# Audio tower with sparsemax attention and top-k experts: one refinement over eight rows, one flag per pair, and a reordered way from the last residual to the first gather

## The chip, the core and the metric

The kernel runs on one core of a Trainium2 chip. The metric is the device time of one launch in microseconds (us), of which three runs are given as a median with their lowest and highest. The engines are called as in the profile: PE (TensorE), DVE (VectorE), ACT (ScalarE), POOL (GpSimd) and SP (SyncE). They run side by side and meet at semaphores.

## What is computed

x is 16 x 64 x 750. Each channel is cut into patches of 200 samples; magnitudes and phases of their spectra go through two dense layers, which gives h, 16 sequences of 256 tokens of width 128. Then:

```python
h = tok(x)                                            # 16 x 256 x 128
h = h + attn(layernorm(h))                            # 8 heads of 64
h = h + ffn(layernorm(h))

def sparsemax(z):                                     # over the 256 scores of a row
    z_sorted = flip(sort(z)); cssv = cumsum(z_sorted)
    k = sum(1.0 + r * z_sorted > cssv)                # r = 1..256: size of the support
    tau = (cssv[k - 1] - 1.0) / k
    return maximum(z - tau, 0.0)

def ffn(x):                                           # 4096 tokens, 8 experts
    probs = softmax(x @ Wr, axis=0)                   # over the tokens
    vals, idx = top_k(probs.T, 1024)                  # 1024 tokens for each expert
    h = gelu(einsum(x[idx], W1) + b1)
    out_e = einsum(h, W2) + b2
    return zeros.at[idx].add(vals * out_e)
```

## The kernel before, in words

**Attention.** The 4096 tokens are worked on in G = 8 groups of 512, that is two sequences. One round of the attention (`attention_round`, one function per engine) does the scores, thresholds and outputs of one group and prepares the next. The order of a round is written out by hand: `PLAN` for PE and ACT, `STEPS` for DVE. A group has 8 score blocks `sc[0]` to `sc[7]`, each 128 x 4 x 256: 128 partitions, 4 rows (two heads by two tiles of tokens), 256 scores. Two blocks make a *pair* d (0 to 3), so a pair holds eight rows per partition, and each block is one *half* u of four rows. There are 32 pairs in all.

For a pair DVE does three steps. `largest` takes the 8 largest scores of each row. `thresholds` takes these out, finds the next 8, sums up the 16, and gets from them the threshold `tau` (128 x 8). In most places the first `largest` instructions of the following pair are laced into it (`laced_thresholds`). This `tau` is right if no more than 16 scores of the row lie above it. A row where the 16th largest score lies above `tau` may need more. `thresholds` therefore ends with three instructions (L1099 to L1102, or L1068 to L1071): a compare into `above`, and two reduces into `more`, one flag for each half and one for the pair. POOL takes the maximum of the three over the partitions (`anymore`, L457), which goes to `more_all`. The third step, `settle` (L1184), loads the pair's flag into a register. If it is zero, DVE goes straight to `minus_tau` (L1205), for which ACT waits before its relu (L646); PE transposes the result of the relu (L829, "turn"). If the flag is not zero, `refine` chooses a half by the flag of half 1, copies its four thresholds to `tau_u`, and `surplus` (L1108) adds up relu(score - tau) over each of the four rows, takes the largest sum over all partitions, and sets `go` if it is over 1 by more than 3e-6. The sum of both half flags stands in `go_5`, so that `go` is also set when both halves are flagged. If `go` is set, `rest` does a Newton step (`newton`: counts the scores above tau, corrects tau, calls `surplus` again), repeats it while `go` is set, copies the thresholds back, and if both halves are flagged goes over the other half with `passes`:

```python
v.tensor_tensor(go_5[0:1, 4:5], more_all[0:1, d, 0:1], more_all[0:1, d, 1:2], ALU.add)
u = v.value_load(more_all[0:1, d, 1:2], min_val=0, max_val=1)
```

**From the last residual to the first gather.** The last group's second norm (`second_norm`, `layernorm`), on DVE with one power on POOL, sends `xn2` to PE, which makes the router's logits. DVE then does the softmax over tokens with POOL, fills some constants (L1319 to L1324), and finds for each expert the 1024th largest probability by 15 steps of two bits (`two_bits`), each with a trip to PE that counts (`total`). A last `total` counts the elements above the threshold (`gt`); `ranks` goes to PE twice, for the elements equal to it (`eq`) and for the chosen ones (`sel`). `one_hots` makes from an expert's ranks a matrix `lo_hot` (128 x 32 x 128) and `hi_val`, PE multiplies them (`expert_slots`, L911), and `slots` turns the product into token numbers `gather_at` and weights `slot_w`.

**Experts.** POOL gathers 1024 rows for an expert by eight indirect DMAs (L506) and adds its results into the output by eight more (L519); the order on its queue is gather 0, 1, 2, scatter 0, and then in turn. PE does the two dense layers (L933, L947), ACT the gelus, DVE the bias and the weights (`weighted`). SP loads the experts' weights before.

## Time and profile before

| | us |
|---|---|
| median of 3 runs (lowest to highest) | 903.33 (898.98 to 903.69) |
| the profiled execution | 908.21 |
| its span | 906.4 |
| PE busy in it | 682.0 (75%) |
| DVE busy | 605.2 (67%) |
| ACT busy | 456.9 (50%) |
| POOL busy | 207.0 (23%) |

The span runs from the first to the last instruction of the execution that was profiled. "Busy" adds up the instructions of one engine. Of all these shares none says what a stage waits for; that is read from the waits and the timeline of each stage. In the rows below, a number in square brackets is the time in which the engine did nothing before the instruction, with the one that ended it; "issue" means that the profile shows nothing that was waited for. Times of a timeline count from the span's start.

### The profile page before, as it was taken

How to read it: one execution, taken by the hardware profiler on the slowest of the kernel's cores; microseconds unless marked ns; L12 is line 12 of the kernel's file. 1: busy time of each engine (PE TensorE's matmuls, PEld its weight loads, DVE VectorE, ACT ScalarE, POOL GpSimd, SP SyncE). 2: the span in 40 equal slices, each digit the busy share in tenths (PEclk: the TensorE clock that was granted, in tenths of full speed). 3: DMA queues.
4: the chain of work that ended last, by engine and by line, in shares of the span. 5: the costliest groups of instructions: out<-in, count | busy, mean ns of one | idle time of the engine just before them, and what ended most of it. 6: DMA issues, size and time to landing. Idle time of an engine off the chain costs nothing. (4 is left out here: it accounts for less than half of the span.)

```text
span 906.4 us, 13135 instructions
## 1 busy us (share of the span) xinstructions
PE 682.0 (75%) x4060; PEld 449.3 (50%) x4060; DVE 605.2 (67%) x2215; ACT 456.9 (50%) x664; POOL 207.0 (23%) x212
## 2 busy tenths in 40 slices
PE   5598679679989997499999998663322996667890
PEld 3254265356565574275575765452211665544570
DVE  2868887588868868788877889846888455432110
ACT  3958638357766764478778777652000231222120
POOL 1000010001000010010010010002005588888776
PEclk9889989889999999699999998895555897779895
DMA  5200000000000000000000000005001153344333
GB/s 156 80 1 1 1 1 1 1 2 13 2 3 13 2 2 13 2 2 13 2 13 3 1 13 1 13 1 157 0 0 33 38 87 43 63 69 69 68 33 29
DMA packets 34722, 23.69 MB, mean 26 GB/s; under 512 B 8232, under 2 KB 31226, under 8 KB 34628
## 3 DMA queue, kind: packets, MB, share of 16 engines
q0 software_dynamic: 11264, 8.40, 6.9%
q1 hardware_dynamic: 23152, 14.21, 5.6%
q8 instruction: 28, 0.46, 0.2%
q14 instruction: 66, 0.54, 0.2%
q10 hardware_dynamic: 212, 0.08, 0.0%
HBM read 14.29 MB, written 8.39 MB: 25 GB/s over the span
## 5 line engine op out<-in xcount | busy, mean ns | idle before, releaser
L549 ACT ACTIVATE front<-ps 128x1024 f32<-128x1024 f32 x128 | 127.8, 1026 | 37.2 <-PE ps L796 13.3
L646 ACT ACTIVATE front<-front,minus_tau 128x256 f32<-128x256 f32 x256 | 108.6, 497 | 57.6 <-DVE minus_tau L1205 56.4
L549 ACT ACTIVATE back<-ps 128x1024 f32<-128x1024 f32 x72 | 73.7, 1024 | 82.6 <-PE ps L920 68.5
L457 POOL CROSS_LANE_REDUCE more_all<-more 128x3 int32<-128x3 f32 x32 | 15.2, 475 | 429.0 <-DVEq L1103 290.9
L829 PE MATMUL ps<-ident,front 128*128 128x128 f32 x512 | 77.0, 300 | 47.4 <-ACTq L648 22.9
L519 POOL DMA_INDIRECT out_dram<-back x64 | 102.6, 1603 | 27.4 <-issue 20.2
L549 ACT ACTIVATE back<-ps,back 128x1024 f32<-128x1024 f32 x32 | 35.4, 1114 | 130.2 <-remote 59.3
L829 PEld LDWEIGHTS ps<-ident,front 128*128 128x128 f32 x512 | 65.0, 154 | 70.2 <-issue 37.4
L947 PE MATMUL ps<-back 128*128 128x128 f32 x512 | 68.4, 300 | 22.3 <-ACT back L549 20.3
L506 POOL DMA_INDIRECT back<-rows,back x64 | 63.5, 992 | 75.6 <-issue 71.3
L947 PEld LDWEIGHTS ps<-back 128*128 128x128 f32 x512 | 66.2, 214 | 26.3 <-issue 26.3
L1077 DVE MATCH_REPLACE8 back<-top,front 128x256 f32<-128x256 f32 x176 | 69.7, 409 | 0.0
L845 PE MATMUL ps<-back,front 128*64 128x256 f32 x512 | 68.5, 396 | 1.3 <-ACT back L549 1.2
L819 PE MATMUL ps<-front 64*128 64x256 f32 x512 | 67.3, 398 | 2.0 <-issue 1.2
L933 PE MATMUL ps<-back 128*128 128x512 f32 x128 | 63.4, 637 | 6.8 <-issue 3.6
L1046 DVE MAX8 top<-front 128x8 f32<-128x256 f32 x168 | 58.7, 413 | 10.0 <-issue 5.9
L1080 DVE MAX8 top<-back 128x8 f32<-128x256 f32 x176 | 59.7, 411 | 1.6
L796 PE MATMUL ps<-xcur,wqkv 128*128 128x512 f32 x128 | 58.7, 611 | 2.0 <-ACT front L572 1.3
L819 PEld LDWEIGHTS ps<-front 64*128 64x128 f32 x512 | 47.5, 191 | 16.5 <-issue 10.2
L751 PE MATMUL ps<-back,w1m 101*128 101x512 f32 x96 | 52.7, 632 | 2.3 <-issue 2.3
L769 PE MATMUL ps<-w2t,hid 128*128 128x128 f32 x384 | 46.9, 284 | 9.1 <-ACT hid_r L607 7.6
L450 POOL TENSOR_TENSOR rstd<-var_eps,minus_half 128x4 f32<-128x4 f32 x16 | 19.5, 1219 | 145.5 <-DVE var_eps L360 145.5
(191 smaller groups left out, 1092.8 us busy)
## 6 DMA issues: line engine op xcount, KB each, us to landing
back<-in_L_ffn_W_dram SPq DMA_DIRECT2D x16, 256.0 KB
front<-in_x_dram SPq DMA_DIRECT2D x4, 750.0 KB, 4.5
rows<-xn SPq DMA_DIRECT2D x8, 256.0 KB, 2.2
out_dram<-h SPq DMA_DIRECT2D x1, 2048.0 KB, 7.8
back<-rows,back POOLq DMA_INDIRECT x64
out_dram<-back POOLq DMA_INDIRECT x64
wqkv<-in_L_attn_W_qkv_dram SPq DMA_DIRECT2D x1, 768.0 KB, 6.0
back<-in_L_ffn_b_dram SPq DMA_DIRECT2D x8, 64.0 KB
```

Of the source, the lines that this page charges most:

```text
L506: g.indirect_dma_start(xg[p][:, s, :], None, rows2[:, :], bass.IndirectOffsetOnAxis(ap=gather_at[p][:, s:s + 1], axis=0))\
L519: g.indirect_dma_start(orow[:, :], bass.IndirectOffsetOnAxis(ap=add_at[p][:, s:s + 1], axis=0), y[p][:, s, :], None, compute_op=ALU.add)\
L549: a.activation(dst, ps[s][:, 0:cols], func, **kw).then_inc(sems[f"free{s}"], 1)
L646: a.activation(prob[n % 2][:, r, :], sc[n][:, r, :], ACT.Relu, bias=minus_tau[:, n // 2, n % 2 * 4 + r:n % 2 * 4 + r + 1])
L796: last = mm(o[:, q * 512:(q + 1) * 512], wqkv[:, m * P:(m + 1) * P], xcur[:, :], start=True, stop=True)
L819: last = mm(o[:, a_ * 512 + it * SEQ:a_ * 512 + (it + 1) * SEQ], z[r, hp, b * SEQ + it * P:b * SEQ + (it + 1) * P], z[r, 4 + hp, b * SEQ:( ...
L829: last = nc.tensor.transpose(o[:, a_ * 512 + jb * SEQ + it * P:a_ * 512 + jb * SEQ + (it + 1) * P], prob[n % 2][:, 2 * a_ + it, jb * P:(jb ...
L845: last = mm(o[a_ * DH:(a_ + 1) * DH, hp * SEQ:(hp + 1) * SEQ], v_sb[p][:, 2 * b + jb, hd * DH:(hd + 1) * DH], prob_t[n % 2][:, 2 * a_ + jb ...
L933: last = mm(o[:, q * 512:(q + 1) * 512], ew1[p][:, m * P:(m + 1) * P], xg_t[:, q * 512:(q + 1) * 512], start=True, stop=True)
L947: last = mm(o[:, s * D:(s + 1) * D], eh[:, k, s * P:(s + 1) * P], ew2[p][:, k, :], start=(k == 0), stop=(k == F // P - 1))
L1077: v.match_replace(sc2[:, r, :], top[d % 2][:, r, 0:8], sc[2 * d + r // 4][:, r % 4, :], LOWEST)
L1080: last = v.max(top[d % 2][:, r, 8:16], sc2[:, r, :])
```

## The change

Three things change. (1) The refinement works on all eight rows of a pair at once, on `tau` itself; the half flags, `tau_u`, `twice` and `passes` go, and one flag per pair is made with the compare. `go` now depends on the row sums alone. (2) Between the last residual and the logits, the norm's statistics of the first two tiles are taken before the last residual, and the constants are filled before the wait for the logits. (3) The count of `gt` rides with the first trip of `ranks`; the first expert's `lo_hot` is made last and in four quarters, each of which releases eight matmuls; `slots` writes the token numbers as integers at once and flags them before the weights are added.

```diff
@@ -894,20 +892,26 @@
-total(3 * BITS // 2, [gt])
 for n, m in enumerate((eq, sel)):
     t_.wait_ge(sems["rk_in"], n + 1)
     job = c.job(0)
     o = slot(job)
+    if m is eq:
+        rows = o[:, E * NT:E * (NT + JB)].rearrange("p (r j) -> p r j", j=JB)
+        for j in range(0, NT, JB):
+            mm(rows, ones[:, :], gt[:, :, j:j + JB], start=(j == 0), stop=(j + JB == NT))
     mm(o[:, 0:E * NT], not_before[:, :], m[:, :, :].rearrange("p e j -> p (e j)"), start=True, stop=True)
     done(job, mm(o[:, 512:512 + E * NT], ones[:, :], m[:, :, :].rearrange("p e j -> p (e j)"),
                  start=True, stop=True))

-def expert_slots(e):
-    t_.wait_ge(sems["hot_ok"], e + 1)
+def expert_slots(e, first=False):
+    if not first:
+        t_.wait_ge(sems["hot_ok"], e + 1)
     job = c.job(3)
     o = slot(job)
     for j in range(NT):
+        if first and j % (NT // 4) == 0:
+            t_.wait_ge(sems["hot_quarter"], j // (NT // 4) + 1)
         last = mm(o[:, 0:5 * CT], lo_hot[:, j, :], hi_val[:, j, :, :].rearrange("p v s -> p (v s)"),
                   start=(j == 0), stop=(j == NT - 1))
     done(job, last)
@@ -1096,19 +1098,14 @@
-    v.tensor_tensor(above[:, :], top[d % 2][:, :, 15], tau[:, d, :], ALU.is_gt)
-    v.drain()
-    v.tensor_reduce(more[:, d, 0:2], above[:, :].rearrange("p (u r) -> p u r", r=4), AX.X, ALU.max)
-    v.tensor_reduce(more[:, d, 2:3], above[:, :], AX.X, ALU.max)
+    v.scalar_tensor_tensor(above[:, :], top[d % 2][:, :, 15], 1.0, tau[:, d, :], ALU.mult, ALU.is_gt,
+                           accum_out=more[:, d, :])
     v.drain().then_inc(sems["more_ok"], 1)

-def half(d, u, r):
-    return sc_d[d][:, ds(u, 1), r, :].rearrange("p u n -> p (u n)")
-
-def surplus(d, u):
-
-    for r in range(4):
-        v.scalar_tensor_tensor(sc2[:, r, :], half(d, u, r), tau_u[:, r:r + 1],
+def surplus(d):
+
+    for r in range(8):
+        v.scalar_tensor_tensor(sc2[:, r, :], sc[2 * d + r // 4][:, r % 4, :], tau[:, d, r:r + 1],
                                zero[:, :].to_broadcast([P, SEQ]),
                                ALU.subtract, ALU.max, accum_out=r_sum[:, r:r + 1])
     v.drain()
@@ -1119,18 +1116,18 @@
     v.tensor_reduce(go_s[:, 0:1], go_t[:, :], AX.X, ALU.max)
     v.drain()
     for k in range(4):
-        v.tensor_copy(go_5[0:1, k:k + 1], go_s[32 * k:32 * k + 1, 0:1])
-    v.drain()
-    v.tensor_reduce(go_s[0:1, 0:1], go_5[0:1, :], AX.X, ALU.max)
+        v.tensor_copy(go_4[0:1, k:k + 1], go_s[32 * k:32 * k + 1, 0:1])
+    v.drain()
+    v.tensor_reduce(go_s[0:1, 0:1], go_4[0:1, :], AX.X, ALU.max)
     v.drain()
     v.tensor_scalar(go[0:1, :], go_s[0:1, 0:1], -1.0, 3e-6, ALU.add, ALU.is_gt)
     v.drain()

-def newton(d, u):
-
-    for r in range(4):
-        v.tensor_scalar(sc2[:, 4 + r, :], half(d, u, r), tau_u[:, r:r + 1], None, ALU.is_gt, ALU.add,
-                        accum_out=r_cnt[:, r:r + 1])
+def newton(d):
+
+    for r in range(8):
+        v.tensor_scalar(sc2[:, r, :], sc[2 * d + r // 4][:, r % 4, :], tau[:, d, r:r + 1], None,
+                        ALU.is_gt, ALU.add, accum_out=r_cnt[:, r:r + 1])
     v.tensor_scalar(r_sum[:, :], r_sum[:, :], -1.0, None, ALU.add)
     v.drain()
     v.tensor_scalar(r_cnt[:, :], r_cnt[:, :], 1.0, None, ALU.max)
@@ -1139,44 +1136,24 @@
     v.drain()
     v.tensor_tensor(r_cnt[:, :], r_sum[:, :], r_cnt[:, :], ALU.mult)
     v.drain()
-    v.tensor_tensor(tau_u[:, :], tau_u[:, :], r_cnt[:, :], ALU.add)
-    v.drain()
-    surplus(d, u)
+    v.tensor_tensor(tau[:, d, :], tau[:, d, :], r_cnt[:, :], ALU.add)
+    v.drain()
+    surplus(d)

 def go_on():
     return v.value_load(go[0:1, 0:1], min_val=0, max_val=1) > 0

-def passes(d, u):
-
-    mine = tau[:, d, ds(u * 4, 4)]
-    v.tensor_copy(tau_u[:, :], mine)
-    v.drain()
-    surplus(d, u)
+def rest_of_refinement(d):
+
+    newton(d)
     with v.If(go_on()):
-        with v.Fori(0, 26):
-            with v.If(go_on()):
-                newton(d, u)
-            v.drain()
-        v.tensor_copy(mine, tau_u[:, :])
-        v.drain()
-
-def rest_of_refinement(d, u):
-
-    v.memset(go_5[0:1, 4:5], 0.0)
-    newton(d, u)
-    with v.If(go_on()):
-        newton(d, u)
+        newton(d)
         with v.If(go_on()):
             with v.Fori(0, 24):
                 with v.If(go_on()):
-                    newton(d, u)
+                    newton(d)
                 v.drain()
             v.drain()
-    v.tensor_copy(tau[:, d, ds(u * 4, 4)], tau_u[:, :])
-    v.tensor_tensor(twice[0:1, :], more_all[0:1, d, 0:1], more_all[0:1, d, 1:2], ALU.mult)
-    v.drain()
-    with v.If(v.value_load(twice[0:1, 0:1], min_val=0, max_val=1) > 0):
-        passes(d, 0)
     v.drain()

 settled = Tally(None)
@@ -1186,20 +1163,16 @@
     v.wait_ge(sems["anymore_ok"], c.up("anymore_ok"))
     v.sem_inc(sems["held"], 1)
     n = settled.up()
-    wide = v.value_load(more_all[0:1, d, 2:3])
+    wide = v.value_load(more_all[0:1, d, :])
     hint = ahead.pop()
     if more_follow:
         ahead.append(v.mark_branch_hint_location())
     v.br_ne(wide, 0, f"refine{n}", f"settled{n}").branch_hint(hint)
     with nc.body(f"refine{n}", valid_engines=[mybir.EngineType.DVE]):
-        v.tensor_tensor(go_5[0:1, 4:5], more_all[0:1, d, 0:1], more_all[0:1, d, 1:2], ALU.add)
-        u = v.value_load(more_all[0:1, d, 1:2], min_val=0, max_val=1)
-        v.tensor_copy(tau_u[:, :], tau[:, d, ds(u * 4, 4)])
-        v.drain()
-        surplus(d, u)
+        surplus(d)
         v.br_ne(v.value_load(go[0:1, 0:1], min_val=0, max_val=1), 0, f"rest{n}", f"settled{n}")
     with nc.body(f"rest{n}", valid_engines=[mybir.EngineType.DVE]):
-        rest_of_refinement(d, v.value_load(more_all[0:1, d, 1:2], min_val=0, max_val=1))
+        rest_of_refinement(d)
         v.br(f"settled{n}")
     nc.switch_bb(f"settled{n}")
     v.tensor_scalar(minus_tau[:, d, :], tau[:, d, :], -1.0, None, ALU.mult).then_inc(sems["tau_ok"], 1)
@@ -1297,8 +1270,35 @@
 attention_round(G - 2, ("hid", "emb"))
 attention_round(G - 1, BEFORE, last=True)
 jobs = {(k, n): job for k, n, job in walk(c, END)}
+half_done = h[:, (G - 1) * 4:G * 4, :]
+v.drain()
+for j in range(2):
+    v.bn_stats(stats[:, j, :], half_done[:, j, :])
+v.drain()
+for j in range(2):
+    v.bn_aggr(mv[:, j, :], stats[:, j, :])
 residual(jobs["out", 1], G - 1, 1)
-second_norm(G - 1, v.drain)
+v.drain()
+for j in range(2, 4):
+    v.bn_stats(stats[:, j, :], half_done[:, j, :])
+v.drain()
+for j in range(2, 4):
+    v.bn_aggr(mv[:, j, :], stats[:, j, :])
+v.drain()
+v.tensor_scalar(var_eps[:, :], mv[:, :, 1], EPS, None, ALU.add).then_inc(sems["ve_ok"], 1)
+v.wait_ge(sems["rows_out"], (G - 1) * 16 + 1)
+v.sem_inc(sems["held"], 1)
+v.wait_ge(sems["rstd_ok"], c.up("rstd_ok"))
+for j in range(4):
+    last = v.tensor_scalar(xn2[:, j, :], half_done[:, j, :], mv[:, j, 0:1], rstd[:, j:j + 1],
+                           ALU.subtract, ALU.mult)
+last.then_inc(sems["xn2_ok"], 1)
+v.memset(seg32[:, :, 1:NT], 1.0)
+v.tensor_copy(iota_b[:, :], iota_r[:, :])
+v.memset(seg32[:, :, 0:1], 0.0)
+for k in range(4):
+    v.memset(nexts[:, k, :], k << (BITS - 2))
+    v.memset(steps4[:, k, :], k << (BITS - 4))
 emptied(jobs["logit", 0])


@@ -1362,19 +1356,18 @@
 thr_b = nexts[:, 0, :].bitcast(f32).unsqueeze(2).to_broadcast([P, E, NT])
 v.tensor_tensor(gt[:, :, :], pr[:, :, :], thr_b, ALU.is_gt)
 v.tensor_tensor(eq[:, :, :], pr[:, :, :], thr_b, ALU.is_equal)
-v.drain().then_inc(sems["cnt_in"], 1)
-filled(c.job(0))
-add_up(above_thr[:, :], E)
-v.drain()
-
-v.tensor_scalar(wanted[:, :], above_thr[:, :], -1.0, float(CAP), ALU.mult, ALU.add)

 def ranks(mask):

     v.drain().then_inc(sems["rk_in"], 1)
     filled(c.job(0))
+    if mask is eq:
+        v.tensor_reduce(above_thr[:, :], ps[0][:, E * NT:E * (NT + JB)].rearrange("p (r j) -> p r j", j=JB),
+                        AX.X, ALU.add)
     v.tensor_tensor_scan(flat(rank), flat(seg32), ps[0][:, 512:512 + E * NT], 0.0, ALU.mult, ALU.add)
     v.drain()
+    if mask is eq:
+        v.tensor_scalar(wanted[:, :], above_thr[:, :], -1.0, float(CAP), ALU.mult, ALU.add)
     v.tensor_tensor(flat(rank), flat(rank), ps[0][:, 0:E * NT], ALU.add).then_inc(sems["free0"], 1)
     v.drain()

@@ -1404,9 +1397,6 @@
     v.drain()
     hi = hi_f[:, ds(e, 1), :].rearrange("p e j -> p (e j)")
     va = vals[:, ds(e, 1), :, :].rearrange("p e j n -> p (e j) n")
-    if first:
-        v.tensor_tensor(lo_hot[:, :, :], iota_b[:, :].unsqueeze(1).to_broadcast([P, NT, P]),
-                        lo_e[:, :].unsqueeze(2).to_broadcast([P, NT, P]), ALU.is_equal)
     for j in range(0 if first else NT):
         v.tensor_scalar(lo_hot[:, j, :], iota_b[:, :], lo_e[:, j:j + 1], None, ALU.is_equal)
     v.tensor_tensor(hi_hot[:, :, :], iota_r[:, 1:CT + 1].unsqueeze(1).to_broadcast([P, NT, CT]),
@@ -1414,6 +1404,11 @@
     v.drain()
     v.tensor_tensor(hi_val[:, :, :, :], hi_hot[:, :, :].unsqueeze(2).to_broadcast([P, NT, 5, CT]),
                     va.unsqueeze(3).to_broadcast([P, NT, 5, CT]), ALU.mult)
+    for q in range(4 if first else 0):
+        rows = slice(q * NT // 4, (q + 1) * NT // 4)
+        v.tensor_tensor(lo_hot[:, rows, :], iota_b[:, :].unsqueeze(1).to_broadcast([P, NT // 4, P]),
+                        lo_e[:, rows].unsqueeze(2).to_broadcast([P, NT // 4, P]), ALU.is_equal)
+        v.drain().then_inc(sems["hot_quarter"], 1)
     v.drain().then_inc(sems["hot_ok"], 1)

 def slots(n, p, first=False):
@@ -1422,16 +1417,16 @@
     job = c.job(3)
     free(job, v.tensor_copy(parts[:, :, :].rearrange("p v s -> p (v s)"), filled(job)[:, 0:5 * CT]))
     v.drain()
-    v.scalar_tensor_tensor(slot_f[:, :], parts[:, 0, :], float(P), parts[:, 1, :], ALU.mult, ALU.add)
-    v.tensor_tensor(parts[:, 2, :], parts[:, 2, :], parts[:, 3, :], ALU.add)
-    v.drain()
-    v.tensor_copy(slot_i[:, ds(e, 1), :].rearrange("p e s -> p (e s)"), slot_f[:, :])
     if not first:
         v.wait_ge(sems[f"xg_in{p}"], n * (16 * CT))
-    v.tensor_copy(gather_at[p][:, :], slot_f[:, :])
+    v.scalar_tensor_tensor(gather_at[p][:, :], parts[:, 0, :], float(P), parts[:, 1, :], ALU.mult, ALU.add)
+    v.drain().then_inc(sems["slots_ok"], 1)
+    v.tensor_tensor(parts[:, 2, :], parts[:, 2, :], parts[:, 3, :], ALU.add)
+    v.tensor_copy(slot_i[:, ds(e, 1), :].rearrange("p e s -> p (e s)"), gather_at[p][:, :])
+    v.drain()
     v.tensor_tensor(slot_w[:, ds(e, 1), :].rearrange("p e s -> p (e s)"), parts[:, 2, :], parts[:, 4, :],
                     ALU.add)
-    v.drain().then_inc(sems["slots_ok"], 1)
+    v.drain()

 def weighted(n, p):
     e = n * 2 + p
```

Where the order of instructions changes, it stands here for DVE at a pair's flag and refinement in the second attention round, first before, then now (`MAX` belongs to the next pair, `ISA` are register operations, `TENSOR_LOAD` reads a flag into a register):

```order
L1099 TENSOR_TENSOR above<-top,tau 128x8
L1101 TENSOR_REDUCE more<-above 128x2
L1102 TENSOR_REDUCE more<-above 128x1
L1046 MAX top<-front 128x8 x4
L1189 TENSOR_LOAD more_all
L1192 BRANCH_PREFETCH_HINT
L1193 COMPARE_AND_BRANCH
L1195 TENSOR_TENSOR go<-more_all 1x1
L1196 TENSOR_LOAD more_all
L1196 ISA x2
L1197 ISA
L1197 COPY tau_u<-tau 128x4
```

```order
L1101 SCALAR_TENSOR_TENSOR above,more<-top,tau 128x8
L1050 MAX top<-front 128x8 x4
L1166 TENSOR_LOAD more_all
L1169 BRANCH_PREFETCH_HINT
L1170 COMPARE_AND_BRANCH
L1108 SCALAR_TENSOR_TENSOR back,r_sum<-front,tau,zero 128x256 x8
L1112 TENSOR_REDUCE go_w<-r_sum 128x1
```

The first instruction of the refinement is now the first row's sum, and there are eight of them in a row. The whole of DVE's order has 3750 rows before and 2235 now.

DVE again, from the last residual on, now (before, both residuals stand together, four statistics follow them, and the fills of L1319 to L1324 stand behind the reciprocal of `all_sum`):

```order
L1212 TENSOR_TENSOR h<-h,att 128x256 [waits free0]
L1276 BN_STATS stats<-h 128x6 x2
L1279 BN_AGGR mv<-stats 128x2 x2
L1212 TENSOR_TENSOR h<-h,att 128x256 [waits free0]
L1283 BN_STATS stats<-h 128x6 x2
L1286 BN_AGGR mv<-stats 128x2 x2
L1288 TENSOR_SCALAR var_eps<-mv 128x4
L1293 TENSOR_SCALAR xn<-h,mv,rstd 128x128 [waits rows_out,rstd_ok]
L1293 TENSOR_SCALAR xn<-h,mv,rstd 128x128 x3
L1296 MEMSET front 128x8x31
L1297 CAST front<-iota_r 128x128
```

Half of the statistics now precede the last residual, and the fills precede the wait for the logits.

PE at the trips behind the bisection and at the first expert's slots, before and now:

```order
L889 MATMUL ps<-front,ones 128x64 [waits cnt_in,free0]
L889 MATMUL ps<-front,ones 128x64 x3
L902 MATMUL ps<-front,not_before 128x256 [waits free0,rk_in]
L903 MATMUL ps<-front,ones 128x256
L902 MATMUL ps<-front,not_before 128x256 [waits free0,rk_in]
L903 MATMUL ps<-front,ones 128x256
L911 MATMUL ps<-front 128x40 [waits free3,hot_ok]
L911 MATMUL ps<-front 128x40 x31
```

```order
L902 MATMUL ps<-front,ones 128x64 [waits free0,rk_in]
L902 MATMUL ps<-front,ones 128x64 x3
L903 MATMUL ps<-front,not_before 128x256
L904 MATMUL ps<-front,ones 128x256
L903 MATMUL ps<-front,not_before 128x256 [waits free0,rk_in]
L904 MATMUL ps<-front,ones 128x256
L915 MATMUL ps<-front 128x40 [waits hot_quarter,free3]
L915 MATMUL ps<-front 128x40 x7
L915 MATMUL ps<-front 128x40 [waits hot_quarter]
L915 MATMUL ps<-front 128x40 x7
```

One wait for DVE less ahead of the ranks, and one every eight matmuls at the slots.

## Rows read from the trace of the kernel before

**Rows 1.** Timeline, VectorE, a threshold step: start us, us, engine line op, [idle <-releaser]

```profile
537.52 0.43 DVE L1084 MAX8 top<-front 128x8 f32<-128x256 f32 x1 [2.29 <-ACT front L549]
```

**Rows 2.** Timeline, TensorE: behind the first and the last refinement

```profile
182.48 1.97 PE L829 MATMUL ps<-ident,front 128*128 128x128 f32 x8 [10.07 <-ACTq L648]
...
375.52 1.94 PE L829 MATMUL ps<-ident,front 128*128 128x128 f32 x8 [18.33 <-ACT front L549]
```

**Rows 3.** Timeline, ScalarE: the relu behind the last refinement

```profile
372.48 1.71 ACT L646 ACTIVATE front<-front,minus_tau 128x256 f32<-128x256 f32 x4 [20.43 <-DVE minus_tau L1205]
```

**Rows 4.** Timeline, GpSimd: the first gather and the first scatter

```profile
685.47 1.31 POOL L506 DMA_INDIRECT back<-rows,back  x1 [52.43 <-issue]
...
725.36 1.64 POOL L519 DMA_INDIRECT out_dram<-back  x1 [3.76 <-DVEq L1460]
```

**Rows 5.** Windows, from the first scatter to the last

```profile
725.00:902.00 177.00, 122.19 (x765) 89.54 (x763) 56.25 (x207) 39.15 (x36) 140.78 (x104) 0.84 0.40 59
```

**Rows 6.** Groups by line and shape, VectorE: xcount, busy us, mean ns, idle before

```profile
L1195 DVE TENSOR_TENSOR go<-more_all 1x1 f32<-1x1 int32 x5 | 0.7, 136 | 1.0 <-issue 1.0
L1132 DVE TENSOR_SCALAR_CACHE_REDUCE back<-front,tau_u 128x256 f32 x8 | 3.4, 476 | 0.2
L1111 DVE SCALAR_TENSOR_TENSOR back<-front,tau_u,zero 128x256 f32<-128x256 f32 x32 | 13.6, 481 | 1.2 <-issue 1.0
L1111 DVE DVE_READ_ACCUMULATOR back<-front,tau_u,zero 128x1 f32 x32 | 2.6, 81 | 0.0
L1205 DVE TENSOR_SCALAR minus_tau<-tau 128x8 f32<-128x8 f32 x32 | 5.5, 172 | 28.5 <-issue 25.9 <-POOL more_all L457 1.6
L1408 DVE TENSOR_TENSOR front<-front 128x4096 bf16<-128x4096 bf16 x1 | 4.4, 4425 | 0.1
L1032 DVE TENSOR_TENSOR front<-front 101x1024 f32<-101x1024 f32 x4 | 4.9, 1226 | 0.3
```

**Rows 7.** Timeline, VectorE: the end of the first refinement; the last one

```profile
180.50 0.17 DVE L1205 TENSOR_SCALAR minus_tau<-tau 128x8 f32<-128x8 f32 x1 [2.21 <-issue]
...
351.38 0.13 DVE L1195 TENSOR_TENSOR go<-more_all 1x1 f32<-1x1 int32 x1
...
352.68 0.48 DVE L1111 SCALAR_TENSOR_TENSOR back<-front,tau_u,zero 128x256 f32<-128x256 f32 x1 [0.20 <-issue]
...
353.09 0.48 DVE L1111 SCALAR_TENSOR_TENSOR back<-front,tau_u,zero 128x256 f32<-128x256 f32 x1
...
356.15 0.14 DVE L1126 TENSOR_SCALAR go<-go_s 1x1 int32<-1x1 f32 x1
...
372.27 0.17 DVE L1205 TENSOR_SCALAR minus_tau<-tau 128x8 f32<-128x8 f32 x1 [1.43 <-issue]
```

**Rows 8.** Timeline, VectorE: the flag at the end of a threshold step

```profile
586.74 0.15 DVE L1099 TENSOR_TENSOR above<-top,tau 128x8 f32<-128x8 f32 x1
...
587.42 1.41 DVE L1046 MAX8 top<-front 128x8 f32<-128x256 f32 x4 [0.23 <-issue]
```

**Rows 9.** Timeline, VectorE: from the last norm to the first slots

```profile
609.87 0.87 DVE L355 BATCH_NORM_STATS2 stats<-h 128x6 f32<-128x128 f32 x4
...
617.79 0.42 DVE L1312 TENSOR_REDUCE lg_max<-lg 128x8 f32<-128x256 f32 x1 [4.09 <-ACT lg L619]
...
620.85 0.27 DVE L1319 MEMSET front<- 128x248 f32 x1
...
621.97 0.43 DVE L1326 TENSOR_TENSOR front<-front,all_sum 128x256 f32<-128x256 f32 x1
...
668.10 0.23 DVE L1329 TENSOR_REDUCE above_thr<-ps 128x8 f32<-128x64 f32 x1 [0.58 <-PE ps L889]
...
669.34 0.69 DVE L1376 TENSOR_TENSOR_SCAN front<-front,ps 128x256 f32<-128x256 f32 x1 [0.73 <-PE ps L903]
...
683.48 0.20 DVE L1423 COPY front<-ps 128x40 f32<-128x40 f32 x1 [1.37 <-PE ps L911]
...
684.24 0.16 DVE L1432 TENSOR_TENSOR front<-front 128x8 f32<-128x8 f32 x1
```

29 lines of the change are left out of this document (10 added, 19 removed).

## The prediction

> **What bounds the kernel now.** I read the lists of waits first, then the timeline, one engine at a time, at the places they point to. The run falls into three parts with different limits.
>
> Up to 600 us the attention rounds run. In rounds without a refinement TensorE (PE) sets the pace: VectorE (DVE), in the second half of a threshold step, waits 2.29 us for scores that ScalarE has still to bring out of PSUM [rows 1]. Whatever DVE saves ahead of such a wait is lost in it. After a refinement it is the other way round: PE stands 10.07 us [rows 2] after the first one and 18.33 us after the last one, because DVE holds back `minus_tau` (ScalarE waits 20.43 us for it [rows 3]). From 600 us to the first gather DVE goes alone through logits, bisection, ranks and slots. From the first scatter at 725.36 us [rows 4] GpSimd's own issues fill the time to the end: 140.8 us busy of 177 [rows 5], and the rest is nearly all the 0.30 us between one issue and the next. The first scatter hangs on the first gather through PE, ScalarE and DVE, so an earlier gather moves the end by as much.
>
> **How many refinements, and of what kind.** L1195 runs five times: five refinements. L1132 ran 8 times, four rows each: two Newton steps. L1111 ran 32 times: eight tests of four rows, so five opening ones, two behind the Newton steps, and one of a second half [rows 6]. The inputs are fixed, so I worked out the reference's attention in double precision to see why. Five pairs of 32 have a row whose 16th largest score lies above its threshold: (group, pair) 0,3; 1,0; 2,1; 3,1; 3,2. Only in 0,3 does a row have more than 16 positive entries (18, row sum 0.0185 too large). In the other four the support is 16 exactly and the threshold is already right. Pair 3,2 is flagged in both halves, and before the change this alone forces its slow path: the sum of the two half flags stands in `go_5`. The new test looks at the row sums only, so there 3,2 ends after its first test. Redone in float32 in the kernel's order of operations, six times with scores shaken by 3e-7, no row sum of the four passed 2.7e-6 over one, and after a Newton step none of the five passed 1.2e-6; the limit is 3e-6.
>
> **The change, part by part.**
>
> *Pair 3,2.* From L1195 at 351.38 to `minus_tau` at 372.27: 20.9 us [rows 7]. Now no half is chosen and no threshold copied, so the first row starts where L1195 did, 1.30 us earlier (352.68). Rows follow each other every 0.41 us [rows 7], so four more cost 1.63 us. The last instruction of the test, at 356.15, moves to 356.48, and with its 0.14 and the gap of 1.43 us that lies between a test and `minus_tau` [rows 7], `minus_tau` comes at 358.05. Gain 14.2 us. ScalarE waits for just this and PE for ScalarE: the stall of 18.33 becomes about 4.1, so all of it counts. I assume no gain from a warmer clock: the first eight transposes took 1.97 us behind a stall of 10.07 and 1.94 behind one of 18.33 [rows 2], so length made no difference between these two. **-14.2**
>
> *Pair 0,3.* Test: +1.63 for four rows, -1.0 for the choice of the half (1.30 in pair 3,2, of which some is a gap of the sequencer that need not be as long elsewhere). Newton step: +1.6 for four more counts, +1.63 for its test. At its end the second load and branch (`twice`) go: a gap of 2.21 us before `minus_tau` [rows 7] becomes part of a plain one; with the copy ahead of it I take -1.7. The load of the half's number at the head of the slow path goes, about -0.5, since the same load and the copy take 1.30 us at the head of the test [rows 7]. PE waits, so it all counts: **+1.7**
>
> *The other three*, one test each: +1.63 less about 1.0. 1,0 and 2,1 lie where PE waits for DVE: **+1.2**. 3,1 delays what DVE has slack for: nothing; without that slack +0.5.
>
> *The flag.* Before: compare at 586.74, drain, two reduces, drain, next work at 587.42 [rows 8]. Now one instruction with an accumulator. Not in this trace at 8 elements; its bounds: as cheap as a compare (a gain of 0.30), or compare and accumulator read (0.08 us [rows 6]) fully in a row behind each other (0.10). I take 0.21, nearest the accumulating pair at 256 elements, where the read starts inside the main instruction. Counted where DVE leads: two threshold steps in the start, eight from the first refinement to the third, six from 537.5 us to the end, 16 x 0.21 = **-3.4** (bounds -1.6 and -4.8). The other 16 fall into DVE's waits for scores.
>
> *Last norm.* Half of the four `bn_stats` (0.87 us) and `bn_aggr` goes into the wait before the last residual [rows 9]; 0.20 each for two of the first and 0.07 each of the second: **-0.5**
>
> *Eleven fills.* 620.85 to 621.97 [rows 9], moved to the wait for logits, 4.09 us long [rows 9], with nothing queued behind. **-1.1**; if the wait were gone, nothing.
>
> *The trip to PE.* Before, the sum of `gt` came back at 668.10 and the first ranks at 669.34 [rows 9]; now one trip brings both. It starts where the old one did and carries the old four matmuls and two more, about 0.6 us later than the sum alone; the reduce and one small instruction come behind it. **-0.45** (bounds 0 and -1.2, the whole distance).
>
> *First one-hots.* 4425 ns in one instruction [rows 6]; a quarter has 1024 elements, and such an instruction takes 1226 [rows 6]. Four with drains: 4 x 1.23 + 3 x 0.08 = 5.15, that is 0.7 longer. DVE then waits 1.37 us for PE's 32 matmuls [rows 9]; now only the last eight of them come behind, a quarter of it with the handing over, some 0.45. Net **-0.2**. The Trainium skill, "VectorE: DVE Perf Modes", section "The TRN2 errata — SBUF-src ops pay a fixed extra latency per instruction", speaks against such a split: every instruction pays its fixed part again. By its formula (N+151)/0.96 the quarters cost 0.47 more before drains, and the sum would be the same to 0.05.
>
> *Slots.* The index is written as an integer at once and flagged before the weights are added: from the copy at 683.48 to the end of the last instruction (684.24 + 0.16) it was 0.92 [rows 9], now the copy, a drain and one instruction, some 0.46: **-0.45**. The gather follows at 685.47 [rows 4], and its descriptors do not get cheaper. Slots 1 to 7 gain or lose about 0.1 us on DVE, which waits there for PE or GpSimd anyway.
>
> Sum: -14.2 + 1.7 + 1.2 - 3.4 - 0.5 - 1.1 - 0.45 - 0.2 - 0.45 = **-17.4 us**. The profiled execution took 908.2 (span 906.4), 4.9 above the median of 903.3; it would be 890.8. I give the time on the median: **886**. Its own range, 880 to 890, takes in 898.98 as the lowest run of before.
>
> **The rivals.**
>
> *Jumps become cheaper too (0.18).* DVE idles 25.9 us before `minus_tau` with no releaser [rows 6]. Its program shrinks from 3750 rows to 2235 in the order of instructions, so jumps over the refinement get shorter. About six of these gaps lie where DVE leads; saving 0.7 us each gives -4: 882. Against: in most gaps it may be the load and the branch alone, which stay. The Trainium skill, "Runtime: NRT & Kernel Launch", section "Instruction fetch mechanics", says that a taken branch to a page not held forces a fetch; it gives no time for one. No row here tells a fetch from the load and the branch.
>
> *The gain of 3,2 reaches the end only in part (0.10).* PE or ScalarE is busy when released early, as their next jobs wait for each other. If 4 us are lost there, 890. Against: all queues waited for the same flag.
>
> *3,2 still goes on (0.07).* A row sum is rounded above 3e-6. Then it costs a gap of 1.5, a count of eight (3.3), five small steps and a test of eight, about 11.3 us: 897.
>
> *Slower: rounding trips several pairs (0.03).* The test now covers 1024 row sums, not 512, per pair. Each extra Newton step costs 11.3 us; with the gain of 17.4, two trips leave it slower (+5), four give 886 + 45 = 931. It decides from the second pair on. For it: 2.7e-6 is near the limit. Against: before, four opening tests of halves passed on the chip.
>
> *The change does nothing measurable (0.02)*: if what PE waits for near 375 us is not the flag. 903.
>
> The forecast itself has 0.60. A measurement of this kernel can tell about 0.5% (4.5 us) from no change. The range that holds 8 in 10 takes the first two rivals and the spread of the runs before: 876 to 892. Faster by over 0.5%: 0.94; within: 0.03; slower: 0.03.
>
> **What would show it.** Right: five refinements, 8 rows each, but only one count of eight rows; `minus_tau` of pair 3,2 6 to 7 us after its refinement begins; PE's longest stall in attention about 11 to 12 us, that of the first refinement; from the last residual to the first gather 73.4 us, not 76.1; from first gather to end unchanged. Wrong: more than 8 counts, a stall of 15 us or more at pair 3,2, or gaps before `minus_tau` that change by microseconds.

## The result and the profile after

| | before | after |
|---|---|---|
| median (lowest to highest) | 901.15 us (898.89 to 903.69) | 871.14 us (869.00 to 875.31) |
| ratio, 95% interval | | 0.9672 (0.9621 to 0.9722) |
| span of the profiled execution | 906.4 | 869.9 |
| DVE busy in it | 605.2 | 598.4 |
| mean granted clock | 0.87 | 0.88 |

The change takes 30.0 us off, where 17.4 were forecast; 871 lies below the range of 876 to 892. Both profiles cut into stretches at the same instructions:

| stretch | before | after | difference | forecast |
|---|---|---|---|---|
| start to the first `minus_tau` | 105.4 | 103.9 | -1.5 | within the flag's term |
| first to last of the 32 `minus_tau` | 493.3 | 466.4 | -26.9 | -14.2 +1.7 +1.2 -3.4 |
| last `minus_tau` to last residual | 10.7 | 10.7 | 0 | 0 |
| last residual to first gather | 76.1 | 72.5 | -3.6 | -2.7 |
| first gather to first scatter | 39.9 | 35.9 | -4.0 | 0 |
| first scatter to last issue | 175.3 | 174.7 | -0.5 | 0 |

Three stretches scatter by themselves. The first `minus_tau` of the changed kernel came at 103.9, 99.1 and 104.8 us in three profiles of it. From the last `minus_tau` to the last residual it took 10.7, 13.3 and 13.2 in the same three, and from gather to scatter 35.9, 38.2 and 34.2. Below I therefore compare kernels by the second stretch, 466.4, 468.7 and 467.0 in those three and 493.3 in both profiles of the kernel before; the medians stand beside it. A *step* is the distance from one `minus_tau` to the next and has the number of the one it ends with; pair 3,2 is the 15th of the 32.

The groups of VectorE, after. `xcount | busy us, mean ns | idle before`:

```profile
L1108 DVE SCALAR_TENSOR_TENSOR back<-front,tau,zero 128x256 f32<-128x256 f32 x48 | 20.0, 480 | 0.9 <-issue 0.8
...
L1178 DVE TENSOR_SCALAR minus_tau<-tau 128x8 f32<-128x8 f32 x32 | 5.5, 172 | 18.3 <-issue 17.7
L1409 DVE TENSOR_TENSOR front<-front 128x1024 bf16<-128x1024 bf16 x4 | 4.9, 1223 | 0.4
...
L1129 DVE TENSOR_SCALAR_CACHE_REDUCE back<-front,tau 128x256 f32<-128x256 f32 x8 | 3.3, 477 | 0.9 <-issue 0.9
```

48 tested rows are six tests of eight, where [rows 6] had 32; eight counted rows are one Newton step, as forecast. But the idle time ahead of `minus_tau` fell from 28.5 us [rows 6] to 18.3. The forecast called a change of microseconds there a sign that it is wrong, and it was.

VectorE's timeline in pair 3,2, after, beside [rows 7]:

```profile
341.57 0.47 DVE L1108 SCALAR_TENSOR_TENSOR back<-front,tau,zero 128x256 f32<-128x256 f32 x1
...
346.65 0.14 DVE L1123 TENSOR_SCALAR go<-go_s 1x1 int32<-1x1 f32 x1
348.17 0.17 DVE L1178 TENSOR_SCALAR minus_tau<-tau 128x8 f32<-128x8 f32 x1 [1.38 <-issue]
```

From the begin to `minus_tau` it takes 6.60 us, where 20.9 stood before: 14.3 less, against a forecast of 14.2. ScalarE, released by this, waited 3.77 us where [rows 3] had 20.43:

```profile
348.38 1.70 ACT L644 ACTIVATE front<-front,minus_tau 128x256 f32<-128x256 f32 x4 [3.77 <-DVE minus_tau L1178]
```

TensorE at the places of [rows 2], after:

```profile
180.82 1.97 PE L827 MATMUL ps<-ident,front 128*128 128x128 f32 x8 [10.04 <-ACTq L646]
...
351.42 1.06 PE L827 MATMUL ps<-ident,front 128*128 128x128 f32 x8 [1.67 <-ACT front L547]
```

The stall of 18.33 is down to 1.67, not to 4.1, and the eight transposes behind it take 1.06 us, not 1.94. The windows show the clock behind it. Columns are those of [rows 5], the third number from the end is the granted clock. Before:

```profile
355.00:360.00 5.00, 2.19 (x6) 0.64 (x4) 3.00 (x18) 0.00 (x0) 0.00 (x0) 0.90 0.00 0
360.00:365.00 5.00, 0.00 (x0) 0.00 (x0) 3.65 (x21) 0.00 (x0) 0.00 (x0) 0.50 0.00 0
...
375.00:380.00 5.00, 4.48 (x12) 2.97 (x13) 4.93 (x17) 4.84 (x9) 0.00 (x0) 0.55 0.00 0
```

and after:

```profile
345.00:350.00 5.00, 4.74 (x12) 1.75 (x10) 3.11 (x18) 1.62 (x4) 0.00 (x0) 1.00 0.01 2
350.00:355.00 5.00, 3.58 (x15) 2.18 (x16) 4.93 (x19) 4.67 (x9) 0.00 (x0) 1.00 0.00 0
355.00:360.00 5.00, 5.00 (x39) 3.78 (x37) 4.61 (x21) 3.33 (x6) 0.31 (x1) 1.00 0.02 5
```

Before, TensorE stood from 357 on and was granted 0.50, which is the lower level of 1.2 GHz, from 359 until it had worked again for some 4 us (the microsecond from 379 to 380 has 0.77, the one from 380 on 1.00). After, the clock stays at 1.00, in this profile: `after_again` below is the same kernel, stood 1.98 us here, and was granted 0.81 and 0.85 in the two windows from 345 to 355 us.

### The profile page after: what moved, and what is told of

It is laid out like the page before. It is cut to its first block and busy times, and to the rows that moved or that the text cites. A ratio compares the mean times of both kernels' runs of the same rounds, so it can differ in the third digit from the quotient of the medians.

```text
span 869.9 us, 12968 instructions
## 1 busy us (share of the span) xinstructions
PE 670.8 (77%) x4060; PEld 445.0 (51%) x4060; DVE 598.4 (69%) x2170; ACT 457.3 (53%) x664; POOL 203.9 (23%) x212
## 5 line engine op out<-in xcount | busy, mean ns | idle before, releaser
L517 POOL DMA_INDIRECT out_dram<-back x64 | 100.5, 1570 | 23.8 <-issue 23.5
L455 POOL CROSS_LANE_REDUCE more_all<-more 128x1 int32<-128x1 f32 x32 | 11.5, 358 | 398.5 <-DVEq L1103 265.3
L827 PE MATMUL ps<-ident,front 128*128 128x128 f32 x512 | 73.5, 291 | 31.6 <-ACTq L646 22.8
L827 PEld LDWEIGHTS ps<-ident,front 128*128 128x128 f32 x512 | 62.3, 149 | 54.3 <-ACTq L646 33.3
L504 POOL DMA_INDIRECT back<-rows,back x64 | 66.3, 1036 | 71.4 <-issue 67.8
L951 PE MATMUL ps<-back 128*128 128x128 f32 x512 | 64.2, 290 | 2.2 <-ACT back L547 2.2
L951 PEld LDWEIGHTS ps<-back 128*128 128x128 f32 x512 | 63.7, 208 | 3.5 <-issue 3.5
L937 PE MATMUL ps<-back 128*128 128x512 f32 x128 | 60.8, 623 | 1.3 <-ACT back L547 1.3
L1448 DVE TENSOR_TENSOR ps<-ps,back 128x512 f32<-128x512 f32 x16 | 11.3, 706 | 71.8 <-PE ps L951 71.8
```

The costliest lines, as they stand in the source:

```text
L504: g.indirect_dma_start(xg[p][:, s, :], None, rows2[:, :], bass.IndirectOffsetOnAxis(ap=gather_at[p][:, s:s + 1], axis=0))\
L517: g.indirect_dma_start(orow[:, :], bass.IndirectOffsetOnAxis(ap=add_at[p][:, s:s + 1], axis=0), y[p][:, s, :], None, compute_op=ALU.add)\
L827: last = nc.tensor.transpose(o[:, a_ * 512 + jb * SEQ + it * P:a_ * 512 + jb * SEQ + (it + 1) * P], prob[n % 2][:, 2 * a_ + it, jb * P:(jb ...
L937: last = mm(o[:, q * 512:(q + 1) * 512], ew1[p][:, m * P:(m + 1) * P], xg_t[:, q * 512:(q + 1) * 512], start=True, stop=True)
L951: last = mm(o[:, s * D:(s + 1) * D], eh[:, k, s * P:(s + 1) * P], ew2[p][:, k, :], start=(k == 0), stop=(k == F // P - 1))
```

## The experiments

All kernels are the one before or the one after with the edit shown. Where I say "stretch", it is the one from the first to the last `minus_tau`.

**The two kernels again**, one execution each, for the scatter of one execution.

> The kernel before once more, for its profile alone. Theory A (the 4 us between first gather and first scatter, and 1.5 us in the first 100 us, are a matter of the one execution): the distance from first gather to first scatter is now near 36 us and the time near 899. Theory B (they belong to the kernel): 40 us again and 903 or more.

> The changed kernel once more, for its profile alone: how far two executions of the same program differ, stage by stage. Expected: from last residual to first gather 72.5 us within 1, from first gather to first scatter 35.9 within 0.5 if that distance belongs to the kernel.

905.5 and 873.7 us, stretches 493.3 and 468.7. The stretch repeats to 0.1 us in the one and 2.3 in the other. Of these, 1.7 us are the step to the 19th `minus_tau`, 24.41 us here and 22.74 in the profile above. TensorE's clock had fallen ahead of it, behind a stall little longer than the 1.67 us above:

```profile
347.27 1.21 PE L827 MATMUL ps<-ident,front 128*128 128x128 f32 x8 [1.98 <-ACT front L547]
```

From first gather to first scatter it was 38.2 us in both, so that distance does not belong to the change.

**The forced step alone.** In the kernel before, the sum of the half flags no longer counts. A pair with both halves flagged ends after the test of one, so the other goes untested:

```diff
-v.tensor_tensor(go_5[0:1, 4:5], more_all[0:1, d, 0:1], more_all[0:1, d, 1:2], ALU.add)
+v.memset(go_5[0:1, 4:5], 0.0)
```

> The kernel before, with one edit: the refinement's go no longer counts the two half flags, so pair 3,2 ends after its first test of four rows (its second half goes untested; its threshold is right all the same). Theory A (the forced slow path of pair 3,2 is the largest part, and is worth more than its own length, because a short stall also keeps TensorE at its full clock): minus_tau of pair 3,2 comes 6 us after its refinement begins instead of 20.9, TensorE's stall there falls from 18.33 us to 2 to 4, the granted clock behind it stays above 0.9, and the time falls by 15 to 18 us. Theory B (only the length counts, and the clock falls in any stall): 14 to 15 us less. Theory C (most of the gain was elsewhere): under 12 us less.

895.48 us (891.62 to 895.75), ratio 0.9894 (0.9877 to 0.9910), stretch 483.8: 9.5 less. That is theory C. Taken out by itself from the kernel before, the forced step is worth a third of the gain, not four fifths. In pair 3,2 something else came up:

```profile
355.75 0.17 DVE L1205 TENSOR_SCALAR minus_tau<-tau 128x8 f32<-128x8 f32 x1 [3.92 <-issue]
```

3.92 us of nothing, where the changed kernel has 1.38. With the slow path skipped, the branch goes over it. TensorE stood 5.97 us there, and its clock fell.

**The flag alone.** The changed kernel with the old compare, drain and two reduces, and three columns for GpSimd:

```diff
-v.scalar_tensor_tensor(above[:, :], top[d % 2][:, :, 15], 1.0, tau[:, d, :], ALU.mult, ALU.is_gt,
-                       accum_out=more[:, d, :])
+v.tensor_tensor(above[:, :], top[d % 2][:, :, 15], tau[:, d, :], ALU.is_gt)
+v.drain()
+v.tensor_reduce(more[:, d, 0:2], above[:, :].rearrange("p (u r) -> p u r", r=4), AX.X, ALU.max)
+v.tensor_reduce(more[:, d, 2:3], above[:, :], AX.X, ALU.max)
```

> The changed kernel with the old way to the flags: a compare, a drain and two reduces, three columns for GpSimd to reduce. Theory A (a step is 0.42 us longer so: 0.31 on DVE and 0.10 because GpSimd's answer comes later): distance from one minus_tau to the next in the stretch where DVE leads 10.48 us instead of 10.06, and the time 26.4 of the attention shrinks by some 8 to 10 us, since about 20 steps lie where DVE leads or where the end hangs on it: 7 to 10 us slower than the changed kernel. Theory B (my forecast: 0.21 a step, 16 steps): 3.4 us slower.

883.46 us (881.35 to 888.31), ratio 0.9768 (0.9729 to 0.9807), stretch 476.5: 8 to 10 us above the three profiles of the changed kernel, as theory A had it. Steps led by VectorE repeat every 10.47 us in it and in the kernel before, and every 10.06 in the changed kernel. So the flag is worth 0.41 a step, not 0.21. 18 of the 31 steps are longer by this much (7.3 us together, against `after`); the other thirteen add 2.8, and among them is one of -3.75, the 27th. There the changed kernel gives some of its lead back (27.8 us against 24.0): VectorE waits 5.33 us for ScalarE's `emb`, where it waited 1.19 in `three_flags` and 1.40 in the kernel before. Most of the 0.41 is on VectorE itself, in the changed kernel (against [rows 8]):

```profile
559.12 0.15 DVE L1101 SCALAR_TENSOR_TENSOR above<-top,tau 128x8 f32<-128x8 f32 x1
559.20 0.08 DVE L1101 DVE_READ_ACCUMULATOR above<-top,tau 128x1 f32 x1
559.51 1.40 DVE L1050 MAX8 top<-front 128x8 f32<-128x256 f32 x4 [0.23 <-issue]
...
560.98 0.17 DVE L1178 TENSOR_SCALAR minus_tau<-tau 128x8 f32<-128x8 f32 x1
```

From the compare to the next MAX8 it is 0.39 where [rows 8] has 0.68, a gain of 0.29: the read starts 0.08 us into a main instruction of only eight elements and ends within 0.02 us of it. The other 0.1 comes from GpSimd, whose groups I had not read. With three columns and with one:

```profile
L455 POOL CROSS_LANE_REDUCE more_all<-more 128x3 int32<-128x3 f32 x32 | 15.2, 475 | 411.6 <-DVEq L1107 274.9 <-DVEq L1076 136.7
```

```profile
L455 POOL CROSS_LANE_REDUCE more_all<-more 128x1 int32<-128x1 f32 x32 | 11.5, 358 | 398.5 <-DVEq L1103 265.3 <-DVEq L1074 133.1
```

**The tail alone.** The kernel before with all that the change does behind the last residual, while `thresholds`, the flags and the refinement stay as they were. In terms of the changed kernel:

```diff
-go_4 = sb("go_4", [P, 4])
+go_5 = sb("go_5", [P, 5])
...
-            def surplus(d):
+            def surplus(d, u):
```

> The kernel before in its attention, the changed one from the last residual on. Theory A: 3 to 3.6 us less, all of it between the last residual and the first gather (72.5 us instead of 76.1). Theory B (the part behind the first gather gained too, 4.6 us in the profiles of before and after, because of the change): 7 to 8 us less, and 36 instead of 40 us from first gather to first scatter. If that distance is 40 us with the new tail or 36 with the old one, the 4 us are a matter of the execution and not of the change.

903.81 us (901.39 to 907.08) against 905.33, ratio 0.9987 (0.9969 to 1.0004); from the last residual to the first gather 72.85, where the kernel before took 76.10 and 75.83. The stretch from residual to gather shortens by 3.0 to 3.3, and the median shows 1.5 of it, with an interval from 0.4 us slower to 2.8 faster. From gather to scatter this run took 39.6 us with the new tail, so theory B is out; whether the rest is lost or only hidden in the scatter is open. One part was run by itself, the first one-hots in one instruction again, in the changed kernel:

```diff
-                for q in range(4 if first else 0):
-                    rows = slice(q * NT // 4, (q + 1) * NT // 4)
...
-                    v.drain().then_inc(sems["hot_quarter"], 1)
+                if first:
+                    v.tensor_tensor(lo_hot[:, :, :], iota_b[:, :].unsqueeze(1).to_broadcast([P, NT, P]),
+                                    lo_e[:, :].unsqueeze(2).to_broadcast([P, NT, P]), ALU.is_equal)
```

> The changed kernel, with the first expert's lo_hot in one instruction ahead of the rest, as before. Theory A (what the profile of the change shows: from the copy of the ranks to the copy of the product 7.98 us in quarters and 7.96 in one piece): the distance stays at 7.96 and the time is the same. Theory B (my forecast): 0.2 us longer in one piece.

72.52 us from residual to gather, where three profiles of the changed kernel have 72.51, 72.86 and 72.75: the four quarters are worth nothing that shows.

**Twice the test.** The changed kernel with the test at the head of every refinement run twice, the second over the first:

```diff
                 with nc.body(f"refine{n}", ...
                     surplus(d)
+                    surplus(d)
```

> The changed kernel, with the first test of each of the five refinements done twice (eight row sums and the reduction to one number, about 5.1 us more for each). Theory A (a stall of TensorE beyond some length also takes its clock down): TensorE's stall at pair 3,2 becomes 6 to 7 us instead of 1.67, the clock behind it falls below 0.8, and the whole is 4 x 5.1 = 20 us slower, plus 2 to 4 us of half clock, less what slack takes up (pair 3,1). Theory B (no clock effect): 15 to 20 us slower, with the clock behind pair 3,2 at 1.00.

911.8 us, 38 above the 873.7 of `after_again`, stretch +34.6: more than either theory said. Five more tests of some 5.3 us are 26.5 us; the remaining 8 are clock and idle, not split further. PE now stands 15.34, 12.95, 6.13, 3.62 and 9.03 us behind the five refinements, and behind the last the clock is at 0.50, as theory A had it. `minus_tau` of pair 3,2 has a gap of 3.66 us and that of the 7th pair one of 2.27, neither of which the changed kernel has. So a microsecond added to a refinement cost 1.3 here, part of it through gaps that came up elsewhere.

**Length added.** The changed kernel with four more copies of `newton` that no pair runs (VectorE's program 3483 rows instead of 2235):

```diff
                 newton(d)
                 with v.If(go_on()):
                     newton(d)
+                    newton(d)
+                    newton(d)
+                    newton(d)
+                    newton(d)
```

> The changed kernel with four more Newton steps written out in a branch that is never taken in this data, so that DVE's program is about as long as before (3483 rows against 2235 and 3750). Theory A (jumps over a long block cost time when its end is not at hand): the gaps before minus_tau without a refinement, which the changed kernel has at 2 places in the rounds and the one before at 7, come back, 1 to 2.5 us each, and the time rises by 3 to 6 us. Theory B (the gaps have nothing to do with the length): within 1.5 us of the changed kernel.

877.87 us (871.62 to 883.21), ratio 0.9679 (0.9615 to 0.9742): the times alone decide nothing. But the stretch is 472.6, 4 to 6 above the changed kernel, and idle times of 2.40 and 2.13 us stand ahead of two `minus_tau` where it has none. By the stretch that is theory A. TensorE stood 1.70 us in pair 3,2, as long as in the changed kernel (1.67), and yet its clock fell to 0.50 and the eight transposes took 1.77 us:

```profile
355.05 1.77 PE L827 MATMUL ps<-ident,front 128*128 128x128 f32 x8 [1.70 <-ACT front L547]
```

**Length taken away.** What no pair of this input runs is left out. In the kernel with the flag zeroed these are `passes` (its call becomes a drain), the second `newton` and the loop; in the changed kernel the last two:

```diff
                 newton(d)
                 with v.If(go_on()):
-                    newton(d)
-                    with v.If(go_on()):
-                        with v.Fori(0, 24):
-                            with v.If(go_on()):
-                                newton(d)
-                            v.drain()
-                        v.drain()
+                    v.drain()
```

> The kernel before without the forced step, as the run with the flag zeroed, and with the code that no pair of this input runs left out: the whole of `passes`, the second `newton` and the loop after it, in all 32 refinements (VectorE's program 2118 rows instead of 3750; what is executed is the same instruction for instruction). It leaves out what pairs would need that do not settle in one step. Theory, the length of VectorE's program costs: 4 to 8 us faster than the run with the flag zeroed (ratio to before 0.980 to 0.985, where that one had 0.989), and the idle stretches of 2.3 to 3.9 us in the refinements (head of the slow path in pair 0,3; between the rows of the tests; ahead of minus_tau of pair 3,2) shrink below 1 us at most places. Rival, the gain that is left over comes from testing eight rows instead of four: 0.989 again, and the same idle stretches at the same places.

869.7 us (868.09 to 877.33), ratio 0.9670 (0.9631 to 0.9709), stretch 466.6. **The same instructions run as in the kernel with the flag zeroed** (24 tested rows, 4 counted, in both), and the stretch is 17.2 us shorter, two to four times what I expected. The seven idle times of 2 us or more are gone; six of them stood inside the stretch and had 17.7 us. This kernel has the old flag, four rows at a time and the old tail, and is as fast as the changed one, although it leaves out what other inputs would need. The groups ahead of `minus_tau`, long and short:

```profile
L1205 DVE TENSOR_SCALAR minus_tau<-tau 128x8 f32<-128x8 f32 x32 | 5.5, 172 | 31.5 <-issue 30.3
```

```profile
L1199 DVE TENSOR_SCALAR minus_tau<-tau 128x8 f32<-128x8 f32 x32 | 5.5, 172 | 18.8 <-issue 17.8
```

Three more runs, on the changed kernel; `after_two` keeps the whole computation:

```diff
                 newton(d)
                 with v.If(go_on()):
-                    newton(d)
-                    with v.If(go_on()):
-                        with v.Fori(0, 24):
...
+                    with v.Fori(0, 25):
```

> The changed kernel with the second `newton` and the loop left out in all 32 refinements (VectorE's program 1371 rows instead of 2235; executed instructions the same but for nothing that counts). It leaves out refinement beyond one step. Theory, length costs: 2 to 5 us faster than the changed kernel in the same comparison. Rival: within 1.5 us of it, since the changed kernel's program already lies below the length at which idle stretches appear.

> The changed kernel with one copy of `newton` fewer: after the first step the loop follows at once, with 25 passes instead of 24, so the computation is whole. VectorE's program has 1851 rows instead of 2235. Theory, length costs: 1 to 3 us faster than the changed kernel, between it and the one with the rest left out. Rival: within 1.5 us of it.

> The changed kernel itself, in the same comparison as the three runs on the program's length: 869 to 875 us, ratio to before 0.964 to 0.970. Minus_tau of the first to of the last pair 466 to 469 us, as in the two profiles there are of it.

| kernel | VectorE rows | idle of 2 us or more with no releaser | stretch | ratio to before |
|---|---|---|---|---|
| before | 3750 | 7, 19.4 us | 493.3 | 1 |
| before, flag zeroed | 3750 | 7, 21.3 | 483.8 | 0.9894 |
| the same, short | 2118 | 0 | 466.6 | 0.9670 |
| before, short (below) | 2382 | 1, 2.4 | 486.8 | 0.9937 |
| after with 4 more `newton` | 3483 | 6, 16.0 | 472.6 | 0.9679 |
| after | 2235 | 4, 10.5 | 466.4 | 0.9672 |
| after, `after_two` | 1851 | 3, 9.3 | 469.7 | 0.9675 |
| after, short | 1371 | 1, 2.2 | 463.1 | 0.9636 |

(The third column counts VectorE between 98 and 605 us, so one of some 3.5 us ahead of the first `minus_tau` lies outside the stretch.) `after_short` took 869.59 us (864.18 to 870.48) beside 873.75 (868.44 to 875.35, ratio 0.9684) for the changed kernel in `after_repeat`: 4 us by median and by stretch, though the two intervals of the ratios (0.9606 to 0.9667, 0.9653 to 0.9715) touch. `after_two`, with a sixth fewer rows, took 871.10 us (870.02 to 876.71), which cannot be told from it: it lost the idle times inside pairs 0,3 and 2,1 and at a residual, and got 3.69 and 2.31 us ahead of two `minus_tau` that had 1.16 and none. So it is not length as such. Nor is it chance from one execution to the next: the three runs that share the long program's attention (`before`, `before_again`, `before_tail`) have the same seven gaps at the same instructions, and the four that share the changed one (`after`, `after_again`, `after_repeat`, `whole_hot`) the same four. Where a gap falls goes with the program, and the short programs have few. No run here moved code without changing its length, so placement is argued and not tested. In places there is no branch at all; here, in the changed kernel, one stands between the last tested row and the reduce that follows it:

```profile
175.61 0.16 DVE L1112 TENSOR_REDUCE go_w<-r_sum 128x1 f32<-128x8 f32 x1 [2.57 <-issue]
```

I read them as waits for instructions. That is the only reading I have for gaps that move with code that is not run, but no row names the fetch as the releaser. The Trainium skill, "Runtime: NRT & Kernel Launch", section "Instruction fetch mechanics", says that a taken branch to a page outside the two that are held forces a fetch; the gaps at `minus_tau` would fit, but no row shows which page was held. It also says that passing from one page to the next in order is mostly hidden; the 2.57 us above disagree, if that is what they are.

**The fourth corner.** The kernel before with its forced step, and short (32 tested rows, 8 counted, as before). Beside the second `newton` and its loop, the loop in `passes` is out:

```diff
                 with v.If(go_on()):
-                    with v.Fori(0, 26):
-                        with v.If(go_on()):
-                            newton(d, u)
-                        v.drain()
-                    v.tensor_copy(mine, tau_u[:, :])
                     v.drain()
```

> The kernel before with its forced step in place, and the code that no pair of this input runs left out: the second `newton` and the loop after it, and the loop in `passes` (VectorE's program 2382 rows instead of 3750; 32 rows tested and 8 counted, as before). It leaves out what pairs would need that do not settle in one step. Theory, the program's length and the forced step add up: the length is worth what it was without the forced step (20 us) and the forced step what it was with the long program (10 us), so 880 to 884 us, ratio 0.976 to 0.981, and no idle stretch of 2 us or more on VectorE between the first and the last minus_tau but at most one. Rival, the two overlap (the long stretch ahead of minus_tau of pair 3,2 in the run with the flag zeroed was the price of a jump that the forced step didn't pay): 872 to 877 us, ratio 0.968 to 0.972.

896.02 us (889.15 to 899.51), ratio 0.9937 (0.9912 to 0.9962), stretch 486.8. Neither theory: the two don't add up and don't overlap. By the whole stretch it looks as if they help each other:

| stretch, us | long | short | length is worth |
|---|---|---|---|
| forced step | 493.3 | 486.8 | 6.5 |
| none | 483.8 | 466.6 | 17.2 |
| the step is worth | 9.5 | 20.2 | |

Cut at the 14th and the 19th `minus_tau`, it reads otherwise:

| steps, us | before | flag zeroed | before, short | zeroed, short | `three_flags` | after |
|---|---|---|---|---|---|---|
| 1st to 14th | 222.8 | 224.6 | 215.4 | 212.8 | 218.8 | 215.2 |
| 14th to 19th | 98.6 | 87.3 | 99.2 | 81.9 | 84.4 | 81.5 |
| 19th to 32nd | 171.8 | 171.9 | 172.2 | 171.9 | 173.3 | 169.8 |

Around pair 3,2 the forced step is worth 11.3 us in the long program and 17.3 in the short one. So it is the largest part of the gain after all, once no gap stands in its place. 6 of the 10.7 us between 6.5 and 17.2 lie here. 4.4 lie in the first thirteen steps, which run before pair 3,2 is reached. The forced step cannot be their cause; what differs there is where the gaps of the four programs fall. Around pair 3,2, without the forced step, the long program has its 3.92 us gap, the short one 1.35:

```profile
359.00 1.94 PE L829 MATMUL ps<-ident,front 128*128 128x128 f32 x8 [5.97 <-ACT front L549]
```

in the long one, and in the short one

```profile
343.97 1.06 PE L829 MATMUL ps<-ident,front 128*128 128x128 f32 x8 [2.85 <-ACT front L549]
```

Behind the 5.97 us of standing the clock is at the lower level, behind the 2.85 it is not. The windows there, long:

```profile
354.00:359.00 5.00, 0.00 (x1) 0.03 (x1) 3.15 (x17) 2.88 (x6) 0.00 (x0) 0.58 0.01 2
359.00:364.00 5.00, 5.00 (x12) 3.08 (x13) 4.93 (x17) 4.53 (x8) 0.00 (x0) 0.50 0.00 0
```

and short:

```profile
339.00:344.00 5.00, 2.15 (x6) 0.63 (x5) 3.47 (x19) 2.90 (x6) 0.00 (x0) 1.00 0.00 2
344.00:349.00 5.00, 5.00 (x23) 3.04 (x24) 4.93 (x17) 4.84 (x9) 0.00 (x0) 1.00 0.00 0
```

Twelve matmuls in 5 us against 23. Of the 5.4 us between 87.3 and 81.9, 2.5 are the gap and the other 3.0 come later, all in the step to the 19th `minus_tau`. That step shows what the clock is worth: in the changed kernel it took 22.7 us in the four profiles in which the clock stayed at 1.00 behind pair 3,2 (`after`, `after_repeat`, `whole_hot`, `after_short`) and 23.3, 23.5, 24.4 and 25.7 where it fell (`padded`, `three_flags`, `after_again`, `after_two`). The length of the stall alone does not tell which it will be: it stayed behind 1.67, 1.70 and 2.85 us and fell behind 1.70, 1.98 and 3.39. In the first thirteen steps, the short kernel with the forced step has a gap of 2.37 us ahead of one `minus_tau` that its partner doesn't have, and steps in which TensorE sets the pace differ by up to 1 us between the two long kernels. I have not settled these.

## Why the prediction was too small

The forecast's terms for the second stretch, put where they belong, beside what came:

| steps | before | after | difference | forecast |
|---|---|---|---|---|
| 1st to 14th | 222.8 | 215.2 | -7.6 | +1.7 +1.2 -1.7 (8 flags) |
| 14th to 19th | 98.6 | 81.5 | -17.2 | -14.2 |
| 19th to 32nd | 171.8 | 169.8 | -2.0 | -1.3 (6 flags) |

The largest miss is in the first row, far from pair 3,2: the sum had nothing there for code that is not run, which it kept as a rival, and half of what the flag is worth.

- **Pair 3,2, "-14.2".** Right on VectorE: 14.3. Its consequence was cut short at "I assume no gain from a warmer clock". That rested on two stalls, 10.07 and 18.33 us, which both end at the lower clock [rows 2]; the question was what one of 4.1 does. Behind the 1.67 us that it became, the clock stayed at 1.00. The next four steps took 54.5 and 54.2 us in the two profiles of the kernel before and 52.6 in `before_unforced_short`, which has the same flag and the clock at 1.00, so the zero was worth some 2 us; in the pair of kernels above it was 3.0. A stall of 4.1 might have kept nothing of this, as `three_flags` with 4.33 shows. "PE stalls 4.1" also overlooked that TensorE had work for 8.2 us from the refinement's begin (341.57 to 349.75), not 5.8 as before (351.38 to 357.19): VectorE began 0.7 us earlier behind the 14th `minus_tau` (22.56 us against 23.21), and TensorE's work reached 1.7 us further (30.74 against 29.02).
- **The flag, "16 x 0.21 = -3.4" (bounds -1.6 and -4.8).** The term that failed worst by factor. It is 0.41 a step, above the bound of 0.30, since GpSimd's part of it was outside the sum, and VectorE's part was 0.29, at the outer bound. The number of steps was too small as well: 18 in the stretch, not 14, which makes 7.3 us. `three_flags` puts all of it at 8 to 10 us, about twice the outer bound. Part of the rest is the clock: in `three_flags` TensorE stood 4.33 us in pair 3,2, and its eight transposes behind that took 1.94 us, the time of the lower clock, where the changed kernel had 1.67 and 1.06.
- **Jumps, a rival at 0.18 with -4, and nothing in the sum.** This is the step of the forecast that failed: the direction was right, the chance and the price too low. I gave it 0.7 us at six branches. The runs show gaps of 2.1 to 4.5 us that come or go whole, at branches and inside straight code. Leaving out code that is not run was worth 6.5 us of the stretch with the forced step in place and 17.2 without it. The sign was in my rows: 28.5 us ahead of 32 `minus_tau`, one of them 2.21 and one 1.43 [rows 6, 7]. Two values for one load and branch already say that more than these is in it. That the gaps are waits for a jump's target stays unproven.
- **Eight rows, "+1.7" and "+1.2".** As forecast, where no gap disturbs the reading. From the short kernel of the old kind to the short one of the new, the step with pair 0,3 goes from 25.98 to 27.44 us, the one with 1,0 from 16.30 to 16.48, the one with 2,1 from 15.65 to 15.79. With the flag's 0.41, which each of them also saves, that is +1.9 and twice some +0.6.
- **The tail, "-2.7".** -3.6 in the two profiles, -3.0 to -3.3 in `before_tail`. Norm, fills and slots each came as said (0.5, 1.0, 0.45), the trip gave 0.6 instead of 0.45, the one-hots 0 instead of 0.2. 1.0 more lies inside the bisection, whose code is the same.
- **From the first gather on, "unchanged".** -4.6 between the two profiles, which is scatter: 35.9, 38.2 and 34.2 us from gather to scatter after, 39.9 and 38.2 before.

The terms don't add up to 30 to the microsecond: what the code that is not run costs depends on where its gaps fall, and part of what is saved ends in waits, as in the 27th step. What the runs show is that without the forced step and that code the old refinement is as fast as the new kernel. All the rest of the change, flag, eight rows and tail, is worth 3.5 us in the stretch and 3.3 from residual to gather between the two short kernels; by the ratios it is 3 us (0.9670 to 0.9636), and as the intervals overlap and the medians are 869.70 and 869.59 us, the times do not show it.

No kernel here that computes the whole is shown to beat the changed one. `after_short` leaves out all refinement beyond one Newton step. Whether moving that code behind the end of the program gives the same 4 us was not tried.

## What to carry to other kernels

Code that is never run can cost time on the engine that leads: look for idle time without a releaser that is larger at some copies of an instruction than at others, and count the rows that the engine's program has between them. When a wait goes, ask what clock TensorE will have behind what is left of it, and look at several stalls of that size, not at one of the size that goes; here some kept the clock and some did not, so it belongs in the range and not only in the sum. When a small hand-over between engines gets cheaper, sum up both sides of it. When two effects seem to strengthen each other, cut the time before the place where the second can act: what differs there has another cause.

## What was not expected of the hardware

- Idle times on VectorE of 2.2 to 4.2 us with no releaser, that moved or vanished with code that was not executed: 7 of them (21.3 us) at 3750 rows of program, none at 2118, for the same executed instructions. They stood at the same instructions in every profile of one program.
- An accumulating instruction of eight elements with its read took 0.39 us to the next work, where a compare and two reduces took 0.68: the read began 0.08 us behind it.
- GpSimd's reduce across partitions of one column took 0.36 us by its group's mean, with three 0.48.
- TensorE at full clock behind 2.85 us of standing, at half behind 5.97 (and behind 4.33 in `three_flags`), with the same work around them. But no length in between parts the two: the same place had full clock behind 1.67 us (`after`) and 1.70 (`whole_hot`) and lost it behind 1.70 (`padded`) and 1.98 (`after_again`), and at 550 us in `after` the transposes behind 2.73 us took 1.97, at a granted clock of 0.50.
